# Gated layer on one Trainium2 core: decayed queries and keys in 1024-column instructions, five blocks to a pair

## The reference, cut to what matters

```python
q_lat = xn @ Wq.T; k_lat = xn @ Wk.T; v_lat = xn @ Wv.T
q = jnp.einsum('btc,hce->bhte', q_lat, Qc)
v = jnp.einsum('btc,hcd->bhtd', v_lat, Vc)
alpha = jax.nn.sigmoid(xn @ Wa_w.T + Wa_b)          # then split by head: (b, h, t, c)
kn = k_lat / jnp.maximum(jnp.linalg.norm(k_lat, axis=-1, keepdims=True), NORM_EPS)
...
def step(S, inp):
    q_t, k_t, v_t, a_t = inp
    S = a_t[..., None] * S + k_t[:, None, :, None] * v_t[..., None, :]
    o_t = jnp.einsum('bhcv,bhc->bhv', S, q_t)
    return (S, o_t)
...
return out @ Wo.T + residual
```

## Time and profile before

| | before |
|---|---|
| median of three runs (lowest, highest) | 594.78 us (590.97, 595.43) |
| span of the profiled execution | 594.2 us |
| TensorE busy over the span | 478.3 us (80%) |
| VectorE busy | 431.7 us (73%) |
| ScalarE busy | 273.4 us (46%) |
| GpSimd busy | 248.9 us (42%) |
| gated layer in the span | about 326 to 421 us |

### The profile page before, as it was taken

One profiled execution on the slowest core, in us unless ns is written; L12 is line 12 of the kernel. 1 busy time (PEld: TensorE's weight loads), 2 busy tenths in 40 slices (PEclk: granted clock), 3 DMA queues, 4 the chain that ended last, 5 costly groups with the idle time before them and its releaser, 6 DMA issues. The chain is left out here.

```text
span 594.2 us, 11914 instructions
## 1 busy us (share of the span) xinstructions
PE 478.3 (80%) x4082; PEld 361.4 (61%) x4082; DVE 431.7 (73%) x1456; ACT 273.4 (46%) x681; POOL 248.9 (42%) x295
## 2 busy tenths in 40 slices
PE   3888782779679685799898999887779879779994
PEld 1455442555648664777694668765358755369983
DVE  4687968797986846855687999996487748327743
ACT  4599570221213245355412768552335413547741
POOL 3631399456812102455201524340485333616650
PEclk9986895587789877799999999979878989969997
DMA  8300004410000005605200000000471500151113
GB/s 253 109 2 1 1 2 144 122 57 2 1 1 1 1 1 141 142 2 105 40 1 1 2 2 2 1 2 3 165 318 30 121 0 26 52 151 47 46 48 104
DMA packets 27998, 33.37 MB, mean 56 GB/s; under 512 B 4962, under 2 KB 21074, under 8 KB 27427
## 3 DMA queue, kind: packets, MB, share of 16 engines
q1 hardware_dynamic: 26002, 29.13, 16.8%
q0 software_dynamic: 1504, 3.15, 1.6%
q10 hardware_dynamic: 432, 0.33, 0.2%
HBM read 26.44 MB, written 6.16 MB: 55 GB/s over the span
## 5 line engine op out<-in xcount | busy, mean ns | idle before, releaser
L2133 POOL TENSOR_TENSOR ea_scaled_rows<-ea_scaled_rows 128x768 f32<-128x768 f32 (+2 forms) x21 | 24.0, 1142 | 50.7 <-ACT ea_scaled_rows L2047 49.6
L3725 POOL DMA_INDIRECT em_results<-em_y_slot,slot_rows x31 | 29.7, 958 | 28.7 <-DVE em_y_slot L3852 28.1
L288 ACT ACTIVATE norm_log<-norm_var 128x4 f32<-128x4 f32 x20 | 4.1, 205 | 73.6 <-DVE norm_var L269 73.6
L3584 PE MATMUL banks<-em_slotT,em_weights 128*128 128x128 f32 x248 | 35.0, 287 | 2.6 <-ACT em_weights L3473 2.6
L3843 DVE SCALAR_TENSOR_TENSOR em_innerT<-banks,em_bias_of,em_soft 128x128 f32<-128x128 f32 x62 | 18.9, 347 | 23.0 <-ACT em_soft L3667 20.2
L38 PE MATMUL banks<-ea_w_high,ea_x_high 128*128 128x384 f32 x64 | 27.2, 425 | 8.7 <-DVE ea_acc L2224 8.5
L3584 PEld LDWEIGHTS banks<-em_slotT,em_weights 128*128 128x128 f32 x248 | 32.1, 202 | 3.3 <-issue 3.3
L2047 ACT ACTIVATE ea_scaled_rows<-banks,ea_gate 128x192 f32<-128x192 f32 x64 | 23.3, 418 | 18.8 <-PE banks L38 18.6
L2795 POOL TENSOR_TENSOR ga_to_end<-ga_cum 128x512 f32<-128x512 f32 x8 | 9.1, 1137 | 45.0 <-DVE ga_to_mid L2857 45.0
L3667 ACT ACTIVATE em_soft<-banks,em_bias_of 128x128 f32<-128x128 f32 x62 | 19.4, 364 | 12.3 <-PE banks L3584 11.7
L38 PE MATMUL banks<-ea_w_high,ea_x_low 128*128 128x384 f32 x64 | 23.7, 371 | 0.0
(11 more groups left out here) (522 smaller groups left out, 1539.4 us busy)
## 6 DMA issues: line engine op xcount, KB each, us to landing
em_up<-in_em_up SPq DMA_DIRECT2D x3, 1536.0 KB, 10.8
ea_wide<-ea_gates SPq DMA_DIRECT2D x4, 1024.0 KB, 11.7
em_down<-in_em_down SPq DMA_DIRECT2D x3, 768.0 KB, 12.2
em_slots<-slot_rows SPq DMA_DIRECT2D x1, 2108.0 KB, 10.8
w_qkv<-in_w_qkv SPq DMA_DIRECT2D x1, 1536.0 KB, 7.4
slot_rows<-em_slots SPq DMA_DIRECT2D x1, 1360.0 KB, 8.5
cos_half<-in_cos_half SPq DMA_DIRECT2D x1, 1024.0 KB, 7.1
sin_half<-in_sin_half SPq DMA_DIRECT2D x1, 1024.0 KB, 9.3
```

The costliest lines, as they stand in the source:

```text
L2133: step(pool.tensor_tensor(scaled_rows[:, k, 0:n], scaled_rows[:, k, 0:n], scaled_rows[:, k, n:2 * n], ALU.add))
L3584: ins = pe.matmul(s.ps[:, k * P:(k + 1) * P], weights[:, n % NW, k // 2, k % 2 * P:(k % 2 + 1) * P], slotT[:, n], start=True, stop=True, s ...
L3725: pool.indirect_dma_start(core.results[:, :], bass.IndirectOffsetOnAxis(ap=slot_rows[:, s, P:P + 1].bitcast(U32), axis=0), y_slot[:, s % N ...
```

## The change

`cum`, `to_mid` and `to_end` become three parts of one buffer, `sums`. The four products' buffers and the pairs `q_two`, `k_two` become one, `faded`: for queries and keys two versions each, every one of 5 slots of 32 columns per pair. Keys lie in slots 1 to 4, queries in slots 0 to 3; the free slot holds the scaled copy of the outer block (key block 0 in slot 0, query block 3 in slot 4). ScalarE makes both query versions in one exponential of 1024 columns (`cum`, `to_mid`) and both key versions in another (`to_mid`, `to_end`), VectorE multiplies each in one product of 1024 columns, and one product of 256 columns makes both scaled copies. The two unscaled copies go away: the far corner's matmuls read slots 0 and 2 (keys, one each) and slots 2 and 4 (queries, both), so there are 16 with 32 weight columns per group in place of 8 with 64. `cap(g+1)` stands ahead of the scaled product, not behind it. The semaphore counts follow: 5 products and 3 exponentials per group. TensorE waits for both large products before the first matmul of `mid`. The memory taken is the same.

```diff
@@ buffers
-        cum = two("cum", NP, P)
-        to_mid, to_end = two("to_mid", NP, P), two("to_end", NP, P)
+        sums = two("sums", 3, NP, P)
+        cum, to_mid, to_end = (sums[:, :, n] for n in range(3))
         q = two("q", NP, P)
-        q_mid, k_mid = two("q_mid", NP, P), two("k_mid", NP, P)
-        q_in, k_in = two("q_in", NP, P), two("k_in", NP, P)
-        q_two, k_two = two("q_two", NP, 2, BLK), two("k_two", NP, 2, BLK)
+        faded = two("faded", 2 * 2 * NP * (NB + 1) * BLK)
@@ counts
-            return 10 * g - (g + HT - 1) // HT - g // HT
+            return 5 * g - (g + HT - 1) // HT - g // HT
@@ new views, with Q_IN, Q_MID = K_MID, K_IN = range(2)
+        def slots(k):
+            return faded[:, k].rearrange("p (w e h n c) -> p w e h n c", w=2, e=2, n=NB + 1, c=BLK)
+        def keys(k):
+            return slots(k)[:, 0, :, :, 1:].rearrange("p e h n c -> p e h (n c)")
+        def queries(k):
+            return slots(k)[:, 1, :, :, 0:NB].rearrange("p e h n c -> p e h (n c)")
+        def far_keys(k, p):
+            return slots(k)[:, 0, K_IN, p, 0:3:2]
+        def far_queries(k, p):
+            return slots(k)[:, 1, Q_IN, p, 2:5:2]
@@ TensorE, mid
                     pe.wait_ge(products, products_before(g) + 2)
...
-                    pe.wait_ge(products, products_before(g) + 4)
...
-                    pe.wait_ge(products, products_before(g) + 8)
+                    pe.wait_ge(products, products_before(g) + 3)
                     for p in range(NP):
-                        for n in range(2):
-                            ins = pe.matmul(both[n].ps[0:2 * BLK, p * P + 2 * BLK:(p + 1) * P], k_two[own(n), k, p],
-                                            q_two[own(n), k, p], start=True, stop=True, skip_group_check=True)
+                        for e in range(2):
+                            for n in range(2):
+                                ins = pe.matmul(both[n].ps[e * BLK:(e + 1) * BLK, p * P + 2 * BLK:(p + 1) * P],
+                                                far_keys(k, p)[own(n), e], far_queries(k, p)[own(n)], start=True,
+                                                stop=True, skip_group_check=True)
@@ ScalarE, decays
-                    for dst, src, sign in ((q_mid, to_mid, 1.0), (k_mid, to_mid, -1.0), (q_in, cum, 1.0)):
-                        act.activation(dst[:, k], src[:, k], ACT.Exp, scale=sign).then_inc(exps, 1)
+                    act.activation(queries(k), sums[:, k, 0:2], ACT.Exp).then_inc(exps, 1)
                     act.wait_ge(logs_ready, 2 * g + 1)
-                    act.activation(k_in[:, k], to_end[:, k], ACT.Exp, scale=-1.0).then_inc(exps, 1)
+                    act.activation(keys(k), sums[:, k, 1:3], ACT.Exp, scale=-1.0).then_inc(exps, 1)
@@ VectorE, decay
-                    kn = spread(kT[:, g], 1, [P, NP, P])
-                    for n, (dst, src) in enumerate(((q_mid, q[:, k]), (k_mid, kn), (q_in, q[:, k]), (k_in, kn))):
-                        dve.wait_ge(exps, 5 * g + n + 1)
-                        dve.tensor_tensor(dst[:, k], dst[:, k], src, ALU.mult).then_inc(products, 1)
-                    dve.wait_ge(exps, 5 * g + 5)
-                    dve.wait_ge(products, products_before(g) + 4)
+                    ks, qs = keys(k), queries(k)
+                    dve.wait_ge(exps, 3 * g + 1)
+                    dve.tensor_tensor(qs, qs, spread(q[:, k], 1, [P, 2, NP, P]), ALU.mult).then_inc(products, 1)
+                    dve.wait_ge(exps, 3 * g + 2)
+                    kn = spread(spread(kT[:, g], 1, [P, NP, P]), 1, [P, 2, NP, P])
+                    dve.tensor_tensor(ks, ks, kn, ALU.mult).then_inc(products, 1)
+                    if 2 <= g + 1 < NT:
+                        cap(g + 1)
+                    dve.wait_ge(exps, 3 * g + 3)
+                    dve.wait_ge(products, products_before(g) + 2)
...
-                    dve.tensor_tensor(k_two[:, k, :, 0], k_in[:, k, :, 0:BLK],
-                                      spread(sc[:, :, OWN + 1], 2, [P, NP, BLK]), ALU.mult).then_inc(products, 1)
-                    dve.tensor_tensor(q_two[:, k, :, 1], q_in[:, k, :, 3 * BLK:],
-                                      spread(sc[:, :, OWN + 2], 2, [P, NP, BLK]), ALU.mult).then_inc(products, 1)
-                    dve.tensor_copy(k_two[:, k, :, 1], k_in[:, k, :, BLK:2 * BLK]).then_inc(products, 1)
-                    dve.tensor_copy(q_two[:, k, :, 0], q_in[:, k, :, 2 * BLK:3 * BLK]).then_inc(products, 1)
-                    if 2 <= g + 1 < NT:
-                        cap(g + 1)
+                    dve.tensor_tensor(key_and_query(k, 0, NB), key_and_query(k, 1, NB - 1),
+                                      spread(sc[:, :, OWN + 1:OWN + 3].rearrange("p h w -> p w h"), 3,
+                                             [P, 2, NP, BLK]), ALU.mult).then_inc(products, 1)
```

More of the change, by code:

```diff
@@ L2349 @@
 RANGE = 80.0
+Q_IN, Q_MID = K_MID, K_IN = range(2)
 BEFORE, WHOLE, AFTER, OWN, NSC = 0, NB, NB + 1, 2 * NB + 1, 3 * NB + 1
@@ L2457, in blocks, with key_and_query @@
             return ap.rearrange("p h (n c) -> p h n c", c=BLK)
+        def slots(k):
[8 more added lines that the diff above has]
+            return slots(k)[:, 1, Q_IN, p, 2:5:2]
+        def key_and_query(k, key_slot, query_slot):
+            size = NP * (NB + 1) * BLK
+            first = size * K_IN + BLK * key_slot
+            step = size * (2 + Q_IN) + BLK * query_slot - first
+            both = faded[:, k, first:first + 2 * step].rearrange("p (w s) -> p w s", w=2)[:, :, 0:size]
+            return both.rearrange("p w (h n c) -> p w h n c", n=NB + 1, c=BLK)[:, :, :, 0]
         def own(n):
@@ L2551, in mid @@
                     pe.wait_ge(products, products_before(g) + 2)
+                    ks, qs = keys(k), queries(k)
                     for p in range(NP):
                         for n in range(2):
-                            pe.matmul(both[n].ps[:, p * P:(p + 1) * P], k_mid[own(n), k, p], q_mid[own(n), k, p],
+                            pe.matmul(both[n].ps[:, p * P:(p + 1) * P], ks[own(n), K_MID, p], qs[own(n), Q_MID, p],
                                       start=True, stop=True, skip_group_check=True)
-                    pe.wait_ge(products, products_before(g) + 4)
                     for p in range(NP):
@@ L2560, in mid @@
                                 at = both[n].ps[e * BLK:(e + 1) * BLK, p * P + (e + 1) * BLK:p * P + (e + 2) * BLK]
-                                pe.matmul(at, k_in[own(n), k, p, e * BLK:(e + 1) * BLK],
-                                          q_in[own(n), k, p, (e + 1) * BLK:(e + 2) * BLK], start=True, stop=True,
+                                pe.matmul(at, ks[own(n), K_IN, p, e * BLK:(e + 1) * BLK],
+                                          qs[own(n), Q_IN, p, (e + 1) * BLK:(e + 2) * BLK], start=True, stop=True,
                                           skip_group_check=True)
-                    pe.wait_ge(products, products_before(g) + 8)
+                    pe.wait_ge(products, products_before(g) + 3)
                     for p in range(NP):
-                        for n in range(2):
-                            ins = pe.matmul(both[n].ps[0:2 * BLK, p * P + 2 * BLK:(p + 1) * P], k_two[own(n), k, p],
-                                            q_two[own(n), k, p], start=True, stop=True, skip_group_check=True)
-                            if p == NP - 1:
-                                ins.then_inc(both[n].filled, 1)
+                        for e in range(2):
[3 more added lines that the diff above has]
+                                                stop=True, skip_group_check=True)
+                                if p == NP - 1 and e == 1:
+                                    ins.then_inc(both[n].filled, 1)
                     if ends(g):
@@ L2678, in move_q @@
                     if g >= 2:
-                        act.wait_ge(products, products_before(g - 2) + 3)
+                        act.wait_ge(products, products_before(g - 2) + 1)
                     act.copy(q[:, k], s.ps[:, :]).then_inc(s.drained, 1)
@@ L2885, in decay @@
                         ring[f"kt_{g - 2}"].ready(dve)
-                    dve.tensor_tensor(blocks(k_all[:, k]), blocks(k_in[:, k]),
+                    dve.tensor_tensor(blocks(k_all[:, k]), blocks(ks[:, K_IN]),
                                       spread(sc[:, :, AFTER:AFTER + NB], 3, shape), ALU.mult).then_inc(products, 1)
```

9 lines of the change are left out of this document (5 added, 4 removed).

## The result

The changed kernel takes 597.02 us (median of 21 runs, 591.95 to 602.51), the kernel before 593.72 us in the same session (21 runs, 586.67 to 597.87). The ratio is 1.0072 with a 95% interval of 1.0040 to 1.0103: slower, where 0.9 us less was forecast. Ratios here compare only executions within 1.5% of the fastest of their kernel, so this one is not quite the 1.0056 of the two medians. Two later comparisons of the same two programs gave 1.0027 (0.998 to 1.007) and 0.9996 (0.995 to 1.004). So the loss is small and was clear of noise in one comparison of three. The experiments show what the layer's part of it is made of.

The account below looks back on a forecast made before the run. VectorE was taken to set the gated layer's pace, TensorE close behind. VectorE's 5.0 us saving, cut to 0.9 us by held GpSimd steps, with ScalarE and TensorE at nothing, gave 594.8 - 0.9 = 593.9 us, range 589.5 to 597.5.

Parts of the forecast that it names:

- VectorE's price for the instructions: VectorE in decay: fewer, longer products and cap filling a wait save 0.67 us in most groups, 5.0 us over the layer.
- Strides: VectorE's products in the five-block slot layout: changed strides priced at nothing, bounded by 0.01 us.
- GpSimd held under the long products: Gated layer: one small GpSimd step per VectorE product makes scale late, cutting VectorE's gain to 0.9 us; chance 0.50.
- ScalarE: Two 1024-column exponentials for four of 512 per group: priced at nothing, up to 0.4 us in a group without cover.
- TensorE's far matmuls: Far corner in mid: 16 matmuls of 32 weight columns for 8 of 64, 0.58 us per group, so no change.
- tiles don't overlap: Rival: far-corner matmuls on TensorE each cost as one of 64 columns, +0.61 us per group, 596.4 us; chance 0.13.
- The end: Layer's end on TensorE's chain: half clock recurs in the stretch before, and the end comes 0.8 to 0.9 us earlier.
- half clock at the end: Rival: the low-clock stretch falls into 404 to 411 us on TensorE's chain, costing 3.4 us, 597.3 us; chance 0.12.
- The own time: Time around the profiled span: span 594.2 us against a median of 594.78, so about 0.6 us.

Follow-up runs that it names:

- e10: The changed kernel, unchanged, in a third profile: layer 79.7 us, one execution, no ratio.
- e1: The kernel before, unchanged, as second profile and null comparison: ratio 1.003 (0.995 to 1.011), layer 80.4 us.
- e8: The changed kernel with cap(g+1) moved back behind the scaled product: ratio 1.001 against the kernel before, layer 82.4 us.
- e11: The changed kernel with 1024-column VectorE products split into two of 512 and GpSimd's chain cut from 6 small steps to 4: ratio 1.002, layer 74.9 us.
- e15: The same program as e11, run again: ratio 0.987 against the kernel before, layer 77.9 us.
- e2: The changed kernel, unchanged, in a second profile: ratio 1.003 against the kernel before, layer 81.4 us.
- e7: The changed kernel with GpSimd's chain cut from 6 small steps per group to 4: ratio 0.987 against the kernel before, layer 77.8 us.
- e3: The changed kernel with each 1024-column VectorE product issued as two of 512: ratio 0.997 against the kernel before, layer 75.6 us.
- e5: The changed kernel with unread 512-column matmuls on TensorE ahead of back(3) to back(6): ratio 0.996 against the kernel before, layer 79.3 us.
- e6: The kernel before with unread 512-column matmuls on TensorE ahead of back(3), back(4) and back(6): ratio 0.996, layer 80.4 us.
- e16: The program of e11 with one unread 512-column matmul ahead of back(4), back(5) and back(6): ratio 0.991 against the kernel before, layer 77.5 us.
- e12: The kernel before with GpSimd's chain cut from 6 small steps per group to 4: ratio 0.997, layer 81.7 us.

## Why the prediction was wrong, point by point

- **VectorE's price for the instructions: right.** The large products stand at a pitch of 1.15 us (373.34 to 374.49; said: 1.14), the 256-column one at 0.34 (377.01 to 377.35), `cap` fills the wait for the product just written. Strides cost nothing that can be read.
- **GpSimd held under the long products: right, and mis-sized.** The forecast was that VectorE would be 0.94 us earlier after `decay(7)` (0.9 in its text); it is 0.36 (395.66 - 332.09 = 63.57 us after the first product, before 401.85 - 337.92 = 63.93). VectorE's idle for `scale` and `front(2)` is 4.8 us. In group 1 I had `k_all` at +0.34, it is +0.48. Groups 2, 3, 4 and 7 fell short by 0.05 us or less each, groups 5 and 6 by 0.14 and 0.18. For group 6 the reason can be read:

```profile
382.03 0.20 POOL L2826 COPY ga_scale_log<-ga_sums 128x16 f32<-128x16 f32 x1
382.17 0.67 POOL L2827 COPY ga_scale_log<-ga_sums 128x4 f32<-128x4 f32 x1
382.92 2.55 POOL L2829 TENSOR_TENSOR ga_scale_log<-ga_scale_log,ga_sums 128x4 f32<-128x4 f32 x3
...
382.11 0.68 DVE L2920 TENSOR_TENSOR ga_q_all<-ga_faded,ga_scale 128x512 f32<-128x512 f32 x1
```

  I had carried over from before that L2827 slips in ahead of `q_all` (0.19 us at 388.40 there). Now `q_all` starts at 382.11, 0.06 us ahead of it, and holds it for 0.67 us. One more step was held than I counted.
- **ScalarE: right.** Its long exponentials (1.06 us) end before VectorE asks for them: in the changed kernel's first profile VectorE never waits for one, in e10 once, for 0.4 us.
- **TensorE's far matmuls: right side, other price.** Lines 2588 and 2595, which answer to L2561 and L2567 of the earlier trace rows:

```profile
358.36 0.45 PE L2588 MATMUL banks<-ga_faded 64*32 64x32 f32 x32
358.63 0.67 PE L2595 MATMUL banks<-ga_faded 64*32 64x64 f32 x32
359.23 0.66 PE L2606 MATMUL banks<-ident,ga_k_all 128*128 128x128 f32 x4
```

  L2595's 32 records take 0.60 us as forecast (0.58), and L2588, whose form is unchanged, takes 0.27 us instead of 0.38: with no change of weight shape behind it, it hands over sooner. That reason is what I read into it; no run isolates it. Together TensorE saves 0.1 us per group. The rival "tiles don't overlap" falls, and with it the Trainium skill's rule of some 60 cycles per matmul (TensorEngine Tiling (Array Packing), "Instruction Overhead") as a price for this pattern: 16 matmuls took the 0.60 us that 8 had taken.
- **The end: the step that failed.** It read "With waits of like length after the change (my sums give 0.9, 2.0 and more) it recurs, the end moves with VectorE and is 0.8 to 0.9 earlier". The half clock did come, but in two of four profiles 7 us later than in before, on `scores(5)` and `mid(6)`. Before's own stretch, on `back(4)` and `mid(5)`, costs 0.6 us (1.1 in e1); in the late place the same length costs 2.8 us of the changed kernel's layer. By the marks, the changed kernel's first profile is 0.4 us ahead of before at `mid(5)`, gains 0.6 more up to `scores(5)`, and loses 2.6 from there to the end. So the layer was 1.5 us longer and not 0.8 to 0.9 shorter. The rival "half clock at the end" had this mechanism with a chance of 0.12 and a price of 3.4 us; it put the stretch 14 us later and dismissed a shift by 10, and 7 were enough. Why the stretch comes at the one place or the other stays open. The five profiles of the two kernels with no half clock at the layer's start divide by kernel (before early three times, changed late twice), which is some evidence that the change has a part in it, but e8, and e11 beside e15, speak against VectorE's gain as the reason.
- **The own time.** I put 0.6 us around the span, from a profiled execution and a median that were not of the same run; in the runs that give both it is 1.8 (e2: 597.51 and 595.7). It cancels in the difference.
- **The range** of 589.5 to 597.5 holds the median of 597.02. That is the breadth of the range, not a sum that came out: the direction was wrong. Of the 3.3 us between the medians, the layer shows 1.5 at most. The rest is not pinned down. In the profiles the time behind the layer varies by up to 5 us with the granted clock, and the comparisons scatter from 1.000 to 1.007 for one and the same pair of programs, so it may be no effect of the change at all.

## What to carry to other kernels

Before merging vector instructions, look at what another engine slips in between them: where GpSimd gets one step per VectorE instruction, longer instructions lengthen every chain that runs beside them, and fewer steps in that chain are worth more than fewer instructions. Price a half-clock stretch by the work it falls on: here the same 7 us cost 0.6 to 1.1 us in one place and 2.8 in another, and one unchanged program had it in either. Where a kernel has such stretches, ask what each would cost if it came some microseconds earlier or later, give that its own chance in the forecast, and judge by several profiles, marking the stage inside each, not by one.

## What the runs showed that I had not expected

- The distance from `scores(5)` to `scores(6)` has two values: 7.2 to 7.3 us in 11 profiles and 10.0 to 10.3 in 7, never between. The short one doesn't mean one place of the stretch: of the 11, five have it on `back(4)` and `mid(5)`, e7 has it 4 us earlier (from 48.4 us after the first product, `scores(4)` to `scores(5)` taking 10.2 us), and e3, e5, e6, e11 and e16 have no half clock after the first 5 us of the layer.
- The late place isn't the changed kernel's alone: the kernel before had it with the short chain (e12), and its layer was 1.8 us longer.
- The time behind the layer, in code that no run changed, ranges over 8 us (173.6 to 181.6), and it is long where the granted clock behind the layer is low.
- One program's executions range over up to 15.7 us (before: 586.7 to 602.4), with the mean granted clock of an execution of before between 0.863 and 0.895. A change of 4 us in one layer, plain in its profile (e3), is at the edge of what 12 executions can show.
